# The up product of an expert stage in 128 + 64 features, with the last 64 in row tiles

## The chip, the cores and the metric

The kernel runs on one core of a Trainium2 chip. Its time is the device time in microseconds of one execution. The engines are PE (TensorE, with PEld for its weight loads), DVE (VectorE), ACT (ScalarE), POOL (GpSimd) and SP (SyncE, which here only issues DMAs). They run side by side and wait for each other through semaphores.

## The reference

One layer over 16 images, 256 tokens each, 192 features: a tokenizer, attention with 12 heads, and a mixture of 16 experts of which each token uses two. The change touches the mixture alone:

```python
logits = jnp.einsum('bld,ed->ble', x, Wr)
probs = jax.nn.softmax(logits, axis=-1)
top_p, top_idx = jax.lax.top_k(probs, TOP_K)                 # TOP_K = 2
gating = jnp.sum(jax.nn.one_hot(top_idx, N_EXPERTS) * top_p[..., None], axis=-2)
def step(y, params):
    W1e, b1e, W2e, b2e, ge = params                          # 192x768, 768, 768x192, 192
    h = jax.nn.gelu(jnp.einsum('bld,df->blf', x, W1e) + b1e, approximate=False)
    out = jnp.einsum('blf,fd->bld', h, W2e) + b2e
    return (y + ge[..., None] * out, None)
```

All of it is in fp32.

## The kernel before

The program has three parts. The image stage (to about 535 us) runs 16 images through tokenizer, attention and router logits. The routing stage (to about 600 us) sorts the 8192 pairs of token and expert by expert into 79 tiles of 128 rows; each tile belongs to one expert, and its number stands in the table `tab`. `r_new` says whether a tile's expert differs from that of the tile two before, whose weight buffer it takes over. The expert stage (to about 991 us) works through the 79 tiles; a last part adds each token's two results.

The expert stage has no planner. Each engine runs its own written list, and semaphores tie them. For tile t:

- POOL gathers the tile's 128 rows of 192 features from `x2_d` in DRAM into `xt` (L594), and later scatters the results to `pair_d` (L600). Four buffers each.
- SP (`moe_loads`) reads expert number and flag into registers (L309, L315) and issues the loads of w1, b1 (`first`, L320 and L323) and w2, b2 (`second`, L328 and L332) into one of two buffers. With the flag at 0 the DMA moves nothing. `first(t)` waits for the up product of t-2 and `second(t)` for the down product of t-2 and its bias sum.
- PE (`moe_tensor`) transposes the rows (`rows_T`, L380, two halves of 96 features), does the up product (`up`, L391 and L392) and the down product (`down`, L402). Its order is up(t), rows_T(t+1), down(t-1), up(t+1).
- The up product has six chunks of 128 hidden units. Each is two matmuls: 96 features, and 96 features and a row of ones, which brings in the bias b1 that lies below w1 as row 97. Both accumulate into the same place of PSUM.
- ACT applies gelu to all 768 columns at once (L429). DVE copies the transposed rows to SBUF (L545) and adds b2 to the down product (L553).

SP, PE, ACT and DVE run this stage as a loop over four tiles at a time, with some tiles written out ahead of and behind it. DMAs that SP issues share one queue, in order.

Of the kernel before, what the change touches and what calls it, by code (L numbers as in the profile page):

```python
# [15 lines left out]
def vit_tower(nc, x0, x1, x2, w0t, w1t, w2t, b012, wft, bf, idx0, idx1, idx2, w_qkv, w_out, b_out, ln_g, ln_b,  # L16
# [3 lines left out]
    ds = bass.ds  # L20

    P = 128
# [29 lines left out]
    x2_d = nc.dram_tensor("x2_rows", ((NT + 1) * P, E), fp32).ap()  # L52
# [4 lines left out]
    qk_d = nc.dram_tensor("qk_parts", (2, 2, NPART, E, T), bf16).ap()  # L57
    NTOK, FIRST = NT * P, NT * P + P
# [3 lines left out]
    with ctx:  # L62
# [45 lines left out]
        def carve(memory, size):  # L108
# [3 lines left out]
            def part(shape, dt=fp32):  # L112
# [11 lines left out]
                if len(shape) == 2:  # L124
# [59 lines left out]
        padrow = sb("padrow", [P, E])  # L184
# [40 lines left out]
        w1b = [late([KH + 1, 2, FF]) for p in range(2)]  # L225
        w2b = [late([P, FC, E]) for p in range(2)]
        b2b = [late([P, E]) for p in range(2)]
        NB = 4
        xt = [late([P, E]) for b in range(NB)]
# [4 lines left out]
        xtT = [late([KH + 1, 2, P]) for p in range(2)]  # L234
# [7 lines left out]
        H = [BK[:, 2 * p:2 * p + 2, :].rearrange("p b n -> p (b n)")[:, 0:FF] for p in range(2)]  # L242
# [12 lines left out]
                 "out_done").split()  # L255
# [46 lines left out]
        def tile_at(k, n):  # L302

            return k + n // 4, n % 4

        def moe_loads(sp):
            sp.wait_ge(s["r_tab"], 1)
            def expert(t):
                return sp.value_load(tab[0:1, ds(t, 1)], min_val=0, max_val=NE - 1)  # L309

            def fresh(t):

                if isinstance(t, int) and t < 2:
                    return None
                return sp.value_load(r_new[0:1, ds(t, 1)], min_val=0, max_val=1)  # L315

            def first(t, p):
                e, new = expert(t), fresh(t)
                wait_prev(sp, s["m_s1"], t - 1)
                sp.dma_start(w1b[p][0:KH, :, :], ew1[ds(e, 1), :, :].rearrange("a (c p) f -> p (a c) f", p=KH),  # L320
                             cond=new) \
                    .then_inc(s[f"m_wa{p}"], 16)
                sp.dma_start(w1b[p][KH:KH + 1, 1, :], eb1[ds(e, 1), :], cond=new).then_inc(s[f"m_wa{p}"], 16)  # L323

            def second(t, p):
                e, new = expert(t), fresh(t)
                wait_prev(sp, s["m_s2"], t - 1)
                sp.dma_start(w2b[p][:, :, :], ew2[ds(e, 1), :, :].rearrange("a (c p) d -> p (a c) d", p=P),  # L328
                             cond=new) \
                    .then_inc(s[f"m_wb{p}"], 16)  # L330
                wait_prev(sp, s["m_y"], t - 1)
                sp.dma_start(b2b[p][:, :], eb2[ds(e, 1), :].rearrange("a d -> (a d)").partition_broadcast(P),  # L332
                             cond=new) \
                    .then_inc(s[f"m_b{p}"], 16)


            first(0, 0)
            for t in range(2):
                first(t + 1, (t + 1) % 2)
                second(t, t % 2)  # L340
            with sp.Fori(0, (NTILE - 3) // 4) as k:
                for j in range(4):
                    first(4 * k + j + 3, (j + 1) % 2)
                    second(4 * k + j + 2, j % 2)
            second(NTILE - 1, (NTILE - 1) % 2)
# [14 lines left out]
        def moe_tensor(pe):  # L360
# [14 lines left out]
            def rows_T(q, r):  # L375
                t, p = 4 * q + r, r % 2
                pe.wait_ge(s[f"m_x{r}"], 16 * q + 16)
                wait_prev(pe, s["m_xT"], t - 1)
                for c in range(2):
                    last = nc.tensor.matmul(XT[p][0:KH, c * P:(c + 1) * P], xt[r][:, c * KH:(c + 1) * KH],  # L380
# [3 lines left out]
            def up(q, r):  # L384
                t, p = 4 * q + r, r % 2
                pe.wait_ge(s["m_xT"], t + 1)
                pe.wait_ge(s[f"m_wa{p}"], 64 * q + 32 * (r // 2) + 32)
# [8 lines left out]
            def down(q, r):  # L396
                t, p = 4 * q + r, r % 2
                pe.wait_ge(s["m_gelu"], t + 1)
                pe.wait_ge(s[f"m_wb{p}"], 32 * q + 16 * (r // 2) + 16)
                wait_prev(pe, s["m_y"], t - 1)  # L400
                for c in range(FC):
                    last = nc.tensor.matmul(Y[p], hT[p][:, c * P:(c + 1) * P], w2b[p][:, c, :],  # L402
                                            start=(c == 0), stop=(c == FC - 1))
                last.then_inc(s["m_s2"], 1)

            rows_T(0, 0)
            rows_T(0, 1)
            up(0, 0)
            up(0, 1)
            rows_T(0, 2)  # L410
            down(0, 0)
            with pe.Fori(0, (NTILE - 3) // 4) as k:
                for j in range(4):
                    up(*tile_at(k, j + 2))
                    rows_T(*tile_at(k, j + 3))
                    down(*tile_at(k, j + 1))
            up(*tile_at(0, NTILE - 1))
            down(*tile_at(0, NTILE - 2))
            down(*tile_at(0, NTILE - 1))

        def moe_scalar(act):
# [3 lines left out]
            def gelu(q, r):  # L425
                t, p = 4 * q + r, r % 2
# [4 lines left out]
            for t in range(3):  # L431
                gelu(0, t)
            with act.Fori(0, (NTILE - 3) // 4) as k:
                for j in range(4):
                    gelu(*tile_at(k, j + 3))

        def moe_vector(dve):
# [12 lines left out]
            for p in range(2):  # L450
                V.memset(xtT[p][KH:KH + 1, :, :], 1.0)
# [20 lines left out]
            V.tensor_copy(r_pad[:, :], padid_i[:, :])  # L472
            V.tensor_copy(r_id[:, 0, :], tokid_i[:, :])
# [37 lines left out]
            for c in range(PAIRS // CG):  # L511
                b, at = c % 2, slice(c * CG, (c + 1) * CG)
                if c == 2:
# [5 lines left out]
                    V.tensor_tensor(r_new[:, 2:NTILE], r_tf[:, 2:NTILE], r_tf[:, 0:NTILE - 2], ALU.not_equal)  # L519
# [21 lines left out]
            def rows_T(q, r):  # L541
                t, p = 4 * q + r, r % 2
                dve.wait_ge(s["m_tr"], t + 1)
                wait_prev(dve, s["m_s1"], t - 1)
                V.tensor_copy(xtT[p][0:KH, :, :], XT[p][0:KH, 0:2 * P].rearrange("p (c t) -> p c t", c=2)) \  # L545
                    .then_inc(s["m_xT"], 1)

            def biased(q, r):
                t, p = 4 * q + r, r % 2
                dve.wait_ge(s["m_s2"], t + 1)  # L550
                dve.wait_ge(s[f"m_b{p}"], 32 * q + 16 * (r // 2) + 16)
                wait_prev(dve, s[f"m_sc{r}"], 16 * q)
# [840 lines left out]
```

## Time and profile before

| | |
|---|---|
| median of 3 runs | 1026.74 us (1025.71 to 1027.69) |
| profiled execution | 1025.64 us, its span 1023.8 us |
| PE busy | 841.7 us, 82% |
| PEld busy | 716.0 us, 70% |
| DVE, ACT, POOL busy | 384.2, 289.1, 398.3 us |
| chain that ended last, largest shares | L402 13%, L391 9%, L392 9% |

The page cuts the span into 40 slices of 25.6 us. PE's digits are 9 (90% or more busy) in slices 6 to 19 and 25 to 38: most of the image stage, and the expert stage. The granted clock is 9 in tenths in both and 5 in the routing stage between them. Queue 1 holds SP's DMAs (84.49 MB), queue 0 POOL's (17.90 MB), and the two instruction queues brought 31 packets of program code, 0.38 MB, for 0.1% of the 16 DMA engines' time. Instructions on PE overlap: a matmul's duration in a row is longer than the distance to the next start, and it is the distances that fill the stage.

### The profile page before, as it was taken

Reading aid. Unit: us, or ns where it says so; the run is one execution under the profiler, and the core shown is the slowest. Engines: PE = TensorE matmul, PEld = TensorE weight load, DVE = VectorE, ACT = ScalarE, POOL = GpSimd, SP = SyncE. Lnnn points to the kernel's source line nnn. Section 1 sums busy time; section 2 is a strip of 40 time slices with the busy share of each in tenths; the row PEclk is TensorE's granted clock in tenths of the full one; section 3 lists DMA queues with packets and bytes.
Section 4 is the critical chain, followed back from the end, with each engine's and each line's share of the span. In section 5 each row is a group of like instructions: output and inputs, shape, how many; then the busy total and the mean of one; then the engine's idle time right before and its main releaser. Section 6 shows DMA issues by size and latency. Waiting matters only on the chain. (4 is left out here: it accounts for less than half of the span.)

```text
span 1023.8 us, 19480 instructions
## 1 busy us (share of the span) xinstructions
PE 841.7 (82%) x6395; PEld 716.0 (70%) x6396; DVE 384.2 (38%) x816; ACT 289.1 (28%) x466; POOL 398.3 (39%) x585
## 2 busy tenths in 40 slices
PE   0047899999999999999740879999999999999970
PEld 0025566666666666676430879999999999999960
DVE  3000355555555555556439911111111111111118
ACT  0011455555555555555310001111111111111110
POOL 7720234444444444444330533433443344334410
PEclk9999999999999999999855569999999999999995
DMA  7203233333333333333011227252367655465129
GB/s 216 34 5 72 70 73 74 73 73 72 72 72 72 72 72 72 72 70 73 1 77 46 75 58 202 69 142 73 104 166 190 169 157 169 120 187 167 42 62 330
DMA packets 83517, 102.78 MB, mean 100 GB/s; under 512 B 14639, under 2 KB 69152, under 8 KB 83294
## 3 DMA queue, kind: packets, MB, share of 16 engines
q1 hardware_dynamic: 74334, 84.49, 31.6%
q0 software_dynamic: 9152, 17.90, 6.3%
q8 instruction: 16, 0.26, 0.1%
q14 instruction: 15, 0.12, 0.0%
HBM read 139.67 MB, written 25.17 MB: 161 GB/s over the span
## 5 line engine op out<-in xcount | busy, mean ns | idle before, releaser
L391 PE MATMUL BK<-shared 96*128 96x128 f32 x948 | 185.0, 276 | 0.7 <-issue 0.6
L392 PE MATMUL BK<-shared 97*128 97x128 f32 x948 | 184.4, 276 | 0.0
L429 ACT ACTIVATE shared<-BK 128x768 f32<-128x768 f32 x79 | 64.0, 810 | 385.1 <-PE BK L392 385.1
L402 PE MATMUL BK<-shared 128*128 128x192 f32 x948 | 168.0, 325 | 1.1 <-DMA shared<-ew 1.1
L600 POOL DMA_INDIRECT pair_rows<-shared x79 | 78.0, 987 | 217.2 <-DVE shared L553 212.9
L402 PEld LDWEIGHTS BK<-shared 128*128 128x128 f32 x948 | 153.1, 190 | 1.4 <-DMA shared<-ew 1.4
L391 PEld LDWEIGHTS BK<-shared 96*128 96x128 f32 x948 | 148.5, 192 | 1.7 <-issue 0.8
L392 PEld LDWEIGHTS BK<-shared 97*128 97x128 f32 x948 | 144.9, 192 | 0.0
L1136 DVE TENSOR_REDUCE negmax<-BK 128x6 f32<-128x1536 f32 x64 | 112.1, 1751 | 10.8 <-PE BK L792 10.6
L545 DVE COPY shared<-BK 96x256 f32<-96x256 f32 x79 | 33.3, 421 | 203.7 <-PE BK L380 203.7
L1011 ACT ACTIVATE shared<-BK 128x1536 f32<-128x1536 f32 x64 | 92.6, 1446 | 24.4 <-PE BK L813 24.2
L594 POOL DMA_INDIRECT shared<-x_rows,shared x79 | 76.7, 971 | 30.2 <-issue 23.8
L553 DVE TENSOR_TENSOR shared<-BK,shared 128x192 f32<-128x192 f32 x79 | 28.2, 357 | 129.4 <-PE BK L402 129.4
L1109 DVE COPY hr<-BK 128x384 f32 (+1 forms) x16 | 8.9, 557 | 170.3 <-PE BK L754 170.3
L824 PE MATMUL BK<-shared,v 128*32 128x256 f32 x768 | 69.1, 385 | 3.9 <-ACT oT L1017 2.4
L772 PE MATMUL BK<-x1T,wqkv 96*96 96x256 f32 x256 | 67.0, 408 | 5.5 <-DVE shared L1128 4.5
L714 PE MATMUL BK<-ident,xs 16*96 16x16 f32 (+1 forms) x192 | 18.9, 224 | 58.5 <-POOL xs L1261 57.8
L792 PE MATMUL BK<-shared 96*128 96x256 bf16 x384 | 54.6, 280 | 6.3 <-DVE negmax L1136 4.0
L714 PEld LDWEIGHTS BK<-ident,xs 16*96 16x96 f32 (+1 forms) x192 | 13.8, 125 | 64.2 <-issue 62.6
L772 PEld LDWEIGHTS BK<-x1T,wqkv 96*96 96x96 f32 x256 | 41.8, 174 | 21.3 <-DVE shared L1128 8.3
L813 PE MATMUL BK<-shared 99*128 99x256 bf16 x384 | 53.3, 275 | 0.9 <-ACT shared L1011 0.9
L792 PEld LDWEIGHTS BK<-shared 96*128 96x128 bf16 x384 | 35.1, 100 | 25.6 <-DVE negmax L1136 10.7
(153 smaller groups left out, 1143.1 us busy)
## 6 DMA issues: line engine op xcount, KB each, us to landing
shared<-ew SPq DMA_DIRECT2D x158, 576.0 KB
shared<-qk_parts SPq DMA_DIRECT2D x112, 96.0 KB, 3.3
qk_parts<-shared SPq DMA_DIRECT2D x32, 288.0 KB, 2.9
shared<-eb SPq DMA_DIRECT2D x79, 96.0 KB
shared<-qk_parts SPq DMA_DIRECT2D x16, 288.0 KB, 3.7
shared<-qk_parts SPq DMA_DIRECT2D x16, 192.0 KB, 4.1
x_rows<-xrow SPq DMA_DIRECT2D x1, 3072.0 KB, 8.7
xrow<-pair_rows SPq DMA_DIRECT2D x8, 384.0 KB, 8.2
```

What stands on the lines that cost most here:

```text
L391: nc.tensor.matmul(o, w1b[p][0:KH, 0, c * P:(c + 1) * P], xtT[p][0:KH, 0, :], start=True, stop=False)
L392: last = nc.tensor.matmul(o, w1b[p][:, 1, c * P:(c + 1) * P], xtT[p][:, 1, :], start=False, stop=True)
L402: last = nc.tensor.matmul(Y[p], hT[p][:, c * P:(c + 1) * P], w2b[p][:, c, :], start=(c == 0), stop=(c == FC - 1))
L429: nc.scalar.activation(hT[p][:, :], H[p], ACT.Gelu).then_inc(s["m_gelu"], 1)
L594: nc.gpsimd.indirect_dma_start(xt[t % NB][:, :], None, x2_d, bass.IndirectOffsetOnAxis(t_src[:, t:t + 1], 0)) \
L600: nc.gpsimd.indirect_dma_start(pair_d, bass.IndirectOffsetOnAxis(t_dst[:, t:t + 1], 0), ysum[t % NB][:, :], None).then_inc(s[f"m_sc{t % NB ...
L772: last = nc.tensor.matmul(M0[0:KH, h * T:(h + 1) * T], wqkv[:, c, at:at + KH], x1T[:, c, :], start=(c == 0), stop=(c == 1))
L792: last = nc.tensor.matmul(S[:, a, t * T:(t + 1) * T], qs[p][0:KS, h, t * P:(t + 1) * P], ks[p][0:KS, h, :], start=True, stop=True)
L813: last = nc.tensor.matmul(ST[:, a, t * T:(t + 1) * T], ks[p][:, h, t * P:(t + 1) * P], qs[p][:, h, :], start=True, stop=True)
L824: last = nc.tensor.matmul(M1[32 * a:32 * a + 32, 0:T], v[p][:, t, HU * u + a, :], pT[u % 2][:, a, t * T:(t + 1) * T], start=(t == 0), stop ...
L1011: nc.scalar.activation(pT[u % 2][:, :, :], ST[:, :, :], ACT.Exp).then_inc(s["act_exp"], 1)
L1136: nc.vector.tensor_reduce(negmax[:, :, HU * u:HU * u + HU].rearrange("p t h -> p h t"), S[:, :, :].rearrange("p a (t k) -> p a t k", t=TT) ...
```

## The change

The up product contracts 192 features as 128 + 64 rather than 96 + 97.

- The first 128 features (`w1a`) are one full matmul per chunk, six in all.
- The other 64 features (`w1c`) use half of the array's rows. `w1c` holds them for chunks 0 to 2 on partitions 0 to 63 and for chunks 3 to 5 on partitions 64 to 127. The matmuls go in pairs, one on the upper and one on the lower half of the array (row tiles), into two PSUM banks. To make such a layout loadable, two DMAs at the start of the program write the last 64 rows of every w1 into a table `w1c_d` in DRAM, 3 MB.
- The transposed rows must lie on both halves. So `x2_d` has rows of 256: 192 features and the last 64 once more, stored by two DMAs. The gather fetches 256 values, and each transpose is 128 wide.
- b1 leaves the product. Behind the routing, six small matmuls of b1 (`b1r`) with a one-hot table of the tiles' experts (`b1e`) give `b1t`, 128 x 6 x 79, which stays in SBUF. ACT adds it in the gelu, which is therefore six instructions of 128 columns, since each chunk has its own bias column.
- SP, PE, ACT and DVE have the 79 tiles written out, without loops. SP reads a tile's number and flag once instead of twice.

PE, one tile in the expert stage. Names: L391 and L392 are the two halves of the up product, L380 the transposes, L402 the down product. Before:

```order
L391 MATMUL BK<-shared 128x128
L392 MATMUL BK<-shared 128x128
L377 ISA
L299 REGISTER_ALU [waits m_x3]
L380 MATMUL BK<-ident,shared 96x128 [waits m_xT]
L380 MATMUL BK<-ident,shared 96x128
L399 ISA [waits m_gelu]
L402 MATMUL BK<-shared 128x192 [waits m_y,m_wb1]
L402 MATMUL BK<-shared 128x192 x5
L386 REGISTER_ALU
L391 MATMUL BK<-shared 128x128 [waits m_gelu,m_wa1,m_xT]
L392 MATMUL BK<-shared 128x128
```

Now, with L398 the 128 features, L403 the 64, L388 the transposes and L413 the down product:

```order
L398 MATMUL BK<-shared 128x128 [waits m_gelu,m_wa1,m_xT]
L398 MATMUL BK<-shared 128x128 x5
L403 MATMUL BK<-shared 128x128 x6
L388 MATMUL BK<-ident,shared 128x128 [waits m_xT,m_x0]
L388 MATMUL BK<-ident,shared 128x128
L413 MATMUL BK<-shared 128x192 [waits m_y,m_wb0,m_gelu]
L413 MATMUL BK<-shared 128x192 x5
L398 MATMUL BK<-shared 128x128 [waits m_gelu,m_wa0,m_xT]
```

There are twelve matmuls of the up product before and now; they no longer alternate, six of the full array stand first and then six of half the array. The stage's order is otherwise kept.

SP, one tile's loads, L309 and L315 the reads of the table, L320 and L323 w1 and b1, L328 w2, L332 b2. Before:

```order
L309 TENSOR_LOAD shared
L309 ISA x2
L315 ISA
L315 TENSOR_LOAD shared
L315 ISA x2
L299 REGISTER_ALU
L320 ISA [waits m_s1]
L320 DMA shared<-ew 96x2x768
L323 ISA
L323 DMA shared<-eb 1x768
L309 TENSOR_LOAD shared
L309 ISA x2
```

Now, L316 and L317 the reads, L323 and L325 the two parts of w1, L331 w2:

```order
L316 TENSOR_LOAD shared
L316 ISA x2
L317 TENSOR_LOAD shared
L317 ISA x2
L323 ISA [waits m_s1]
L323 DMA shared<-ew 128x768
L325 ISA
L325 DMA shared<-up_rest 128x384
L331 DMA shared<-ew 128x6x192 [waits m_s2]
L335 ISA [waits m_y]
L335 DMA shared<-eb 128x192
```

The second pair of reads between the two halves of the loads is gone, and b1's DMA of one row has become the DMA of `w1c`.

```diff
-    x2_d = nc.dram_tensor("x2_rows", ((NT + 1) * P, E), fp32).ap()
+    x2_d = nc.dram_tensor("x2_rows", ((NT + 1) * P, 2 * P), fp32).ap()
+    KR, HC = E - P, FC // 2
+    w1c_d = nc.dram_tensor("up_rest", (NE, P, FF // 2), fp32).ap()
+    NW = 2
...
-        w1b = [late([KH + 1, 2, FF]) for p in range(2)]
+        w1a = [late([P, FF]) for w in range(NW)]
+        w1c = [late([P, FF // 2]) for w in range(NW)]
...
-        H = [BK[:, 2 * p:2 * p + 2, :].rearrange("p b n -> p (b n)")[:, 0:FF] for p in range(2)]
+        H = [[BK[:, 2 * p + c // HC, c % HC * P:(c % HC + 1) * P] for c in range(FC)] for p in range(2)]
...
+            def first(t, e, new):
+                w = t % NW
+                wait_prev(sp, s["m_s1"], t - NW + 1)
+                sp.dma_start(w1a[w][:, :], ew1[ds(e, 1), 0:P, :].rearrange("a k f -> (a k) f"), cond=new) \
+                    .then_inc(s[f"m_wa{w}"], 16)
+                sp.dma_start(w1c[w][:, :], w1c_d[ds(e, 1), :, :].rearrange("a k f -> (a k) f"), cond=new) \
+                    .then_inc(s[f"m_wa{w}"], 16)
...
+            pe.wait_ge(s["ld_b1"], 16)
+            pe.wait_ge(s["r_hot"], 1)
+            for c in range(FC):
+                last = nc.tensor.matmul(BK[:, 1, c * NTILE:(c + 1) * NTILE], b1r[:, c * P:(c + 1) * P], b1e[:, :],
+                                        start=True, stop=True)
+            last.then_inc(s["pe_b1"], 1)
             pe.wait_ge(s["r_meta"], 1)
+            pe.wait_ge(s["dve_b1"], 1)
...
                 for c in range(FC):
-                    o = H[p][:, c * P:(c + 1) * P]
-                    nc.tensor.matmul(o, w1b[p][0:KH, 0, c * P:(c + 1) * P], xtT[p][0:KH, 0, :], start=True, stop=False)
-                    last = nc.tensor.matmul(o, w1b[p][:, 1, c * P:(c + 1) * P], xtT[p][:, 1, :],
-                                            start=False, stop=True)
+                    nc.tensor.matmul(H[p][c], w1a[w][:, c * P:(c + 1) * P], xtT[p][:, 0, :],
+                                     start=(c % HC == 0), stop=False, skip_group_check=True)
+                for c in range(HC):
+                    for h in range(2):
+                        k = slice(h * KR, (h + 1) * KR)
+                        last = nc.tensor.matmul(H[p][h * HC + c], w1c[w][k, c * P:(c + 1) * P], xtT[p][k, 1, :],
+                                                start=False, stop=True, skip_group_check=True)
                 last.then_inc(s["m_s1"], 1)
...
-                nc.scalar.activation(hT[p][:, :], H[p], ACT.Gelu).then_inc(s["m_gelu"], 1)
+                for c in range(FC):
+                    last = nc.scalar.activation(hT[p][:, c * P:(c + 1) * P], H[p][c], ACT.Gelu, bias=b1t[:, c, t:t + 1])
+                last.then_inc(s["m_gelu"], 1)
...
-            for p in range(2):
-                V.memset(xtT[p][KH:KH + 1, :, :], 1.0)
...
+                    V.tensor_scalar(b1e[:, :], r_tf[0:NE, :], eid[:, 0:1], None, ALU.is_equal).then_inc(s["r_hot"], 1)
...
+            dve.wait_ge(s["pe_b1"], 1)
+            V.tensor_copy(b1t[:, :, :], BK[:, 1, 0:FC * NTILE].rearrange("p (c t) -> p c t", t=NTILE)) \
+                .then_inc(s["dve_b1"], 1)
...
+            sp.dma_start(b1r[:, :], eb1).then_inc(s["ld_b1"], 16)
+            for h in range(2):
+                sp.dma_start(w1c_d[:, h * KR:(h + 1) * KR, :], ew1[:, P:E, h * (FF // 2):(h + 1) * (FF // 2)]) \
+                    .then_inc(s["st_w1c"], 16)
...
-            sp.dma_start(x2_d[0:NT * P, :].rearrange("(p t) e -> p t e", t=NT), xrow[:, :, :]).then_inc(s["st_x2"], 16)
+            rows = x2_d[0:NTOK, :].rearrange("(p t) e -> p t e", t=NT)
+            sp.dma_start(rows[:, :, 0:E], xrow[:, :, :]).then_inc(s["st_x2"], 16)
+            sp.dma_start(rows[:, :, E:2 * P], xrow[:, :, P:E]).then_inc(s["st_x2"], 16)
```

## Rows read from the trace of the kernel before

**Rows 1.** Table by stretches, expert stage: busy us (count) per engine, TensorE clock, DMA share, GB/s.

```profile
620.00:1000.00 380.00, 369.54 (x2873) 368.33 (x2871) 60.62 (x157) 61.52 (x76) 145.85 (x149) 0.99 0.48 135
```

**Rows 2.** List of waits, 599 to 1000 us, PE: us in total, times, longest.

```profile
PE BK L380 <- DMA shared<-x_rows,shared: 5.4, 2, 4.8
PE BK L402 <- DMA shared<-ew: 1.1, 1, 1.1
```

**Rows 3.** Instructions in order of time, one tile: start us, us, instruction, count, [idle before].

```profile
764.54 0.39 PE L391 MATMUL BK<-shared 96*128 96x128 f32 x2
...
767.22 0.38 PE L380 MATMUL BK<-ident,shared 128*96 128x128 f32 x2
...
767.45 2.13 PE L402 MATMUL BK<-shared 128*128 128x192 f32 x12
...
769.41 0.39 PE L391 MATMUL BK<-shared 96*128 96x128 f32 x2
```

**Rows 4.** Instructions in order of time, image stage, PE around L824.

```profile
302.21 0.41 PE L824 MATMUL BK<-shared,v 128*32 128x256 f32 x2
302.26 0.22 PE L737 MATMUL BK<-w2s,x12T 96*16 96x64 f32 x1
302.32 1.03 PE L824 MATMUL BK<-shared,v 128*32 128x256 f32 x10
...
308.48 1.06 PE L824 MATMUL BK<-shared,v 128*32 128x256 f32 x12
309.48 0.83 PE L792 MATMUL BK<-shared 96*128 96x256 bf16 x6
```

**Rows 5.** The same stretch from 303.27 us: three tile shapes in a row, PE and PEld.

```profile
303.27 0.70 PE L744 MATMUL BK<-rr,bd 128*128 128x256 f32 x2
303.90 0.65 PE L745 MATMUL BK<-rr,bd 128*64 128x256 f32 x2
304.48 0.64 PE L714 MATMUL BK<-ident,x2c 128*96 128x128 f32 x4
...
303.90 0.19 PEld L745 LDWEIGHTS BK<-rr,bd 128*64 128x64 f32 x2 [0.33 <-issue]
```

**Rows 6.** The same view, 299 us: PEld where 64 rows follow 128.

```profile
299.12 0.69 PEld L714 LDWEIGHTS BK<-ident,xs 64*96 64x96 f32 x10 [0.20 <-issue]
```

**Rows 7.** The page's groups of instructions: busy us, mean ns of one, idle before.

```profile
L429 ACT ACTIVATE shared<-BK 128x768 f32<-128x768 f32 x79 | 64.0, 810 | 385.1 <-PE BK L392 385.1
...
L545 DVE COPY shared<-BK 96x256 f32<-96x256 f32 x79 | 33.3, 421 | 203.7 <-PE BK L380 203.7
...
L1011 ACT ACTIVATE shared<-BK 128x1536 f32<-128x1536 f32 x64 | 92.6, 1446 | 24.4 <-PE BK L813 24.2
...
L824 PE MATMUL BK<-shared,v 128*32 128x256 f32 x768 | 69.1, 385 | 3.9 <-ACT oT L1017 2.4
```

**Rows 8.** Instructions in order of time: SP's DMA issues, first load, a skipped one, a real one.

```profile
572.14 0.37 SPq L320 DMA_DIRECT2D shared<-ew  x1
...
673.14 0.08 SPq L328 DMA_DIRECT2D shared<-ew  x1
...
763.32 0.33 SPq L320 DMA_DIRECT2D shared<-ew  x1
```

**Rows 9.** The same view, end of routing and first gather.

```profile
587.69 7.25 PE L370 MATMUL BK<-pixels 128*128 128x79 f32 x33
...
596.91 1.07 POOL L594 DMA_INDIRECT shared<-x_rows,shared  x1 [6.43 <-DVE shared L539]
...
599.75 0.64 PE L380 MATMUL BK<-ident,shared 128*96 128x128 f32 x2 [4.81 <-DMA shared<-x_rows,shared]
```

**Rows 10.** Table by stretches: the store of the rows, and a w2b load.

```profile
533.00:541.00 8.00, 1.40 (x7) 1.29 (x7) 5.54 (x11) 1.91 (x2) 0.00 (x0) 0.50 0.92 393
...
679.00:682.00 3.00, 3.00 (x24) 3.00 (x23) 0.42 (x1) 0.81 (x1) 0.97 (x1) 1.00 0.89 257
```

**Rows 11.** Instructions in order of time, start: POOL behind its last gather.

```profile
57.12 0.33 POOL L1260 COPY xs<-pixels 64x192 f32<-64x192 f32 x1 [1.45 <-DMA pixels<-x,i]
```

More of the change, by code:

```diff
@@ L223, in vit_tower @@
         r_new = late([P, NTILE], i32)
-        w1b = [late([KH + 1, 2, FF]) for p in range(2)]
-        w2b = [late([P, FC, E]) for p in range(2)]
-        b2b = [late([P, E]) for p in range(2)]
+        w1a = [late([P, FF]) for w in range(NW)]
+        w1c = [late([P, FF // 2]) for w in range(NW)]
+        w2b = [late([P, FC, E]) for w in range(NW)]
+        b2b = [late([P, E]) for w in range(NW)]
         NB = 4
-        xt = [late([P, E]) for b in range(NB)]
+        xt = [late([P, 2 * P]) for b in range(NB)]
         r_df = late([P, NTILE])
@@ L233, in vit_tower @@
         t_dst = late([P, NTILE], i32)
-        xtT = [late([KH + 1, 2, P]) for p in range(2)]
+        xtT = [late([P, 2, P]) for p in range(2)]
         hT = [late([P, FF]) for p in range(2)]
@@ L299, in wait_prev @@
                 eng.wait_ge(which, count)
-        def tile_at(k, n):
-            return k + n // 4, n % 4
         def moe_loads(sp):
             sp.wait_ge(s["r_tab"], 1)
[L308 to L320, printed above, removed]
-                             cond=new) \
[L322 to L328, printed above, removed]
-                             cond=new) \
[L330 to L345, printed above, removed]
@@ new lines, in moe_loads, with chosen @@
+            sp.wait_ge(s["st_w1c"], 32)
+            def chosen(t):
+                e = sp.value_load(tab[0:1, t:t + 1], min_val=0, max_val=NE - 1)
+                new = None if t < NW else sp.value_load(r_new[0:1, t:t + 1], min_val=0, max_val=1)
+                return e, new
+            def first(t, e, new):
[5 more added lines that the diff above has]
+                    .then_inc(s[f"m_wa{w}"], 16)
@@ new lines, in second @@
+            def second(t, e, new):
+                w = t % NW
+                wait_prev(sp, s["m_s2"], t - NW + 1)
+                sp.dma_start(w2b[w][:, :, :], ew2[ds(e, 1), :, :].rearrange("a (c p) d -> p (a c) d", p=P),
+                             cond=new) \
+                    .then_inc(s[f"m_wb{w}"], 16)
+                wait_prev(sp, s["m_y"], t - NW + 1)
+                sp.dma_start(b2b[w][:, :], eb2[ds(e, 1), :].rearrange("a d -> (a d)").partition_broadcast(P),
+                             cond=new) \
+                    .then_inc(s[f"m_b{w}"], 16)
@@ L347, in moe_loads @@
+            before = chosen(0)
+            first(0, *before)
+            for t in range(1, NTILE):
+                now = chosen(t)
+                first(t, *now)
+                second(t - 1, *before)
+                before = now
+            second(NTILE - 1, *before)
             for b in range(NB):
@@ L378, in rows_T @@
+            def rows_T(t):
+                p, r = t % 2, t % NB
+                pe.wait_ge(s[f"m_x{r}"], 16 * (t // NB) + 16)
                 wait_prev(pe, s["m_xT"], t - 1)
                 for c in range(2):
-                    last = nc.tensor.matmul(XT[p][0:KH, c * P:(c + 1) * P], xt[r][:, c * KH:(c + 1) * KH],
+                    last = nc.tensor.matmul(XT[p][:, c * P:(c + 1) * P], xt[r][:, c * P:(c + 1) * P],
                                             ident[:, :], start=True, stop=True, is_transpose=True)
@@ L394, in up, with down @@
                 last.then_inc(s["m_s1"], 1)
-            def down(q, r):
-                t, p = 4 * q + r, r % 2
+            def down(t):
+                p, w = t % 2, t % NW
                 pe.wait_ge(s["m_gelu"], t + 1)
-                pe.wait_ge(s[f"m_wb{p}"], 32 * q + 16 * (r // 2) + 16)
+                pe.wait_ge(s[f"m_wb{w}"], 16 * (t // NW) + 16)
                 wait_prev(pe, s["m_y"], t - 1)
                 for c in range(FC):
-                    last = nc.tensor.matmul(Y[p], hT[p][:, c * P:(c + 1) * P], w2b[p][:, c, :],
+                    last = nc.tensor.matmul(Y[p], hT[p][:, c * P:(c + 1) * P], w2b[w][:, c, :],
@@ L403, in down @@
                                             start=(c == 0), stop=(c == FC - 1))
                 last.then_inc(s["m_s2"], 1)
[L406 to L417, printed above, removed]
@@ L418, in moe_tensor @@
-            down(*tile_at(0, NTILE - 2))
-            down(*tile_at(0, NTILE - 1))
+            rows_T(0)
+            rows_T(1)
+            up(0)
+            for t in range(1, NTILE):
+                up(t)
+                if t + 1 < NTILE:
+                    rows_T(t + 1)
+                down(t - 1)
+            down(NTILE - 1)
         def moe_scalar(act):
@@ L423, in moe_scalar @@
             nc.scalar.activation(r_p[:, :, :], r_ls[:, :, :], ACT.Exp).then_inc(s["r_exp"], 1)
-            def gelu(q, r):
-                t, p = 4 * q + r, r % 2
+            act.wait_ge(s["dve_b1"], 1)
+            for t in range(NTILE):
+                p = t % 2
                 act.wait_ge(s["m_s1"], t + 1)
                 wait_prev(act, s["m_s2"], t - 1)
-                nc.scalar.activation(hT[p][:, :], H[p], ACT.Gelu).then_inc(s["m_gelu"], 1)
[L431 to L435, printed above, removed]
+                for c in range(FC):
+                    last = nc.scalar.activation(hT[p][:, c * P:(c + 1) * P], H[p][c], ACT.Gelu, bias=b1t[:, c, t:t + 1])
+                last.then_inc(s["m_gelu"], 1)
         def moe_vector(dve):
```

57 lines of the change are left out of this document (28 added, 29 removed).

## The prediction

> **What bounds the kernel now.** I read the table by stretches first, then the PE waits, then one tile in order of time. In the expert stage (620 to 1000 us) PE works 369.5 of 380 us at full clock, while DVE works 60.6 and ACT 61.5 [rows 1]. PE's waits from 599 us on hold 4.8 us for the first row gather and 1.1 us for one weight load, and little else [rows 2]. So PE's own instruction stream sets the stage's end, and a change is worth what it takes from that stream.
>
> One tile is the distance between two up products: 764.54 to 769.41, 4.87 us [rows 3]. It splits by start times. The trace shows two MATMULs for each fp32 product. Twelve up products take from 764.54 to 767.22 = 2.68 us, or 24 instructions of 0.112. The two transposes take 0.23. The six down products take from 767.45 to 769.41 = 1.96 us, or 0.163 per instruction of 192 columns. That is 0.85 ns a column, so 0.109 at 128 columns and 0.218 at 256: a matmul costs its moving columns, whether 96 or 128 rows are filled.
>
> **The up product after the change.** Six products contract 128 features: 12 instructions x 0.112 = 1.34 us. Six more contract the remaining 64, three in array rows 0 to 63 and three in rows 64 to 127, alternating: again 12 instructions. All hangs on whether the two halves run side by side. No matmul of before does this with row tiles, so the cost per instruction lies between 0.112 (one after another) and 0.056 (fully paired).
>
> The nearest row is the probability-times-value product L824, in three column tiles. Its 12 instructions of 256 columns take 1.06 us [rows 4]; one after another they would take 12 x 0.218 = 2.6. With the last one's duration off (0.385, L824's mean [rows 7]), 0.675 us holds three intervals of 0.225: four waves of three. So tiles do run abreast, in full, for fp32. I take full pairing: 6 waves x 0.112 = 0.67 us. The weak point is the weight load. L824 loads 32 columns, here it is 128, and a 128-column load fills the slot (the up stream shows a load per 0.112 as well [rows 3]). If loads of the two row tiles took turns, nothing would be gained.
>
> TensorE: Matmul & The Clock Gate of the Trainium skill (section Packing small matmuls) says that matmuls start and end strictly in program order. Under it the two instructions of one product would come before the other tile's, so that 12 instructions would need 7 slots, 0.11 us a tile more. The trace disagrees for column tiles: two of L824 start at 302.21, the last L737, which stands ahead of them in the program, at 302.26 [rows 4]. I keep six slots.
>
> **The price of changing the tile shape.** It is paid twice a tile now, and nothing in the expert stage paid it before. Rows 5 show it: L744 (128 columns of weights) to L745 (64) to L714 (96). L744's two instructions take 0.70; less 0.385 for the last one, also of 256 columns, that is 0.32 between starts, where the columns need 0.218: 0.10 of weight load in the open. From the second L744 to L745 it is 0.63 - 0.32 = 0.31, again 0.09 to 0.10 over 0.218: the array empties. For L745 to L714: 0.65 - 0.38 = 0.27, then 0.58 - 0.27 = 0.31, the same 0.09 to 0.10. The weight loader's own rows show holes of 0.33 us [rows 5], and 0.20 where a 64-row product follows a 128-row one [rows 6], so the row height counts as a shape too. Into the row tiles: 0.10 + 0.10. Back, to transposes: 0.10 + 0.05 (a matmul of 128 columns lasts 0.39 - 0.112 = 0.28 [rows 3], so L714's four stand (0.64 - 0.28) / 3 = 0.12 apart against 0.112; only the first start carries the open load, 0.03 for 96 columns, and I book 0.05 for 128). Together 0.35 us. Bounds: 0 if row tiles need no emptying, 0.42 if both ways cost the dear 0.21.
>
> TensorEngine Tiling (Array Packing) of the Trainium skill (section Key Properties) says the same without a number, that a change of tiling mode drains the array; by these rows the drain alone is 0.1 us. It also says that tiles load weights and multiply in parallel, which for row tiles no row here shows.
>
> **Sum per tile.** Saved: six slots of 0.112 = 0.67. Added: 0.35. Net 0.32 us, so the period goes from 4.87 to 4.55, and 79 tiles give 25.3 us.
>
> **What hides the rest.**
> - Gelu: one ACTIVATE of 768 columns, 0.81 us, becomes six of 128. From 768 columns at 810 ns and 1536 at 1446 [rows 7] a column is 0.83 ns and the start 0.17 us, so 0.28 each, 1.7 us a tile. ACT has a 4.55 us period, and between up(t) and down(t) lie a transpose pair, down(t-1) and up(t+1), over 4 us. At the last tile only down(77), 1.96 us, covers it. Cost 0 to 0.2.
> - Weight loads: a buffer is refilled after up(t-2). A real load issues in 0.33 us where a skipped one takes 0.08 [rows 8]. One is issued at 763.32 for the product at 769.41 [rows 3, 8]: 6.1 us, of which 576 KB at 257 GB/s [rows 10] need 2.3 and the way there some more. Bytes stay 576 KB (384 + 192). With two TENSOR_LOADs a tile fewer SP issues earlier, so I book 0; bounds -1 (the 1.1 us of rows 2 goes) and +4, a few expert changes exposed.
> - The bias table: six small products (12 instructions) stand behind the last L370. There 33 instructions take 7.25 us, 0.22 each [rows 9] at the lower clock, so 2.6 us. PE has nothing until the first gather lands at 599.75, 4.8 us later [rows 2, 9]. DVE's copy of 474 columns (about 0.7 us, by the 0.42 of 256 columns [rows 7]) ends about 598.4. Hidden, margin 1.3 us; if late, 1 us. One small DVE operation at the third chunk adds 0.2.
> - The rows now go out as pieces of 768 and 256 bytes. Before, 3 MB went in 8 us at 393 GB/s [rows 10]; the 768-byte loads run at 257 GB/s, 334 pieces a us. 8192 pieces are then 25 us, from 533 to 558, and the first weights are issued only at 572.14 [rows 8]. Hidden; if pieces of 256 bytes are twice as dear, the first weights wait, up to 5 us.
> - The start: 3 MB go from DRAM to DRAM behind the constants (from about 11 us). PE waits for POOL's gathers, whose last lands at 57.12 [rows 11]. At 257 GB/s for either direction that is 12 to 25 us, so it ends by 36, and what SP has queued behind it (the second level's detour) by about 50. Cost 0, upper bound 10.
>
> Total: 1025.64 (the profiled execution: 1023.8 span and 1.8 around it) - 25.3 + 0.2 = 1000.5 us. The median of the runs shown is 1.1 above that execution.
>
> **Rivals.**
> 1. Slower: the row tiles don't pair, because their 128-column weight loads take turns at 0.112. Then the up product keeps its 2.68 us and the 0.35 for the shape changes comes on top: 79 x 0.35 = 27.7, so 1053.5 us. It decides from 0.17 us a pair: six pairs of that cost 1.01, and with 0.35 the gain is gone. For it: the load fills its slot already, and L824's loads are a quarter as wide. Against: three L824 loads of different tiles fit beside one wave without a trace of turns. 17 in 100.
> 2. Pairs one slot out of step (strict order, two instructions of one product in a row): 7 slots, +0.11 x 79 = 8.8, 1009 us. Against it speaks the overtaking in rows 4. 6 in 100.
> 3. The gain is met by another bound: weights late at the expert changes (16 experts, two buffers each), or straight-line code of 79 tiles that must be fetched. Before, 31 packets of the instruction queues took 0.1% of 16 engines, 16 us, 0.5 each; 30 more, all waited for, are 16 us. The last image steps are straight-line as well, and PE's slice 19, which lies in them, still reads 9. 1005 to 1025; 6 in 100.
> 4. The mechanism is half as dear as I read (no emptying between row shapes): -0.2 x 79, 985 us. 3 in 100.
>
> My forecast has 68 in 100, with 994 to 1006 as its own range. The stated range is 988 to 1030, which takes in rivals 2 and 3 and leaves out rival 1. A measurement of this kernel tells 0.2%, about 2 us, from no change. Faster 0.81 (all but rival 1 and a stray 2), same 0.02, slower 0.17.
>
> **What the profile after would show.** Right: L403 in pairs, two starts within some 10 ns, waves 0.11 apart; one start distance near 0.2 before the first L403 and another after the last; tile period 4.55; no PE wait on gelu or weights; PE's first matmul still near 57.8. Wrong: L403 starts 0.11 apart one by one (rival 1), or period 4.55 with the stage beginning later than 602, or holes of PE in regular distances of three tiles (code).

## The result and the profile after

The changed kernel takes 1000.68 us (median of 4 runs, 998.83 to 1001.66) against 1026.62 us (4 runs) of the kernel before: ratio 0.9745, 95% interval 0.9728 to 0.9762. The forecast was 1000.5. The profiled execution took 998.83 us with a span of 997.0, 26.8 less than before's.

In the changed kernel L398 is the up product over 128 features and L403 that over the last 64, in row tiles. L388 are the transposes, L413 is the down product, L437 gelu, L552 the copy of the transposed rows, L377 the bias table's product. L323, L325, L331 and L335 are SP's loads of w1a, w1c, w2b and b2b. First PE's waits from 600 us on, then SP's (us in total, times, longest), then SP's in the kernel before (there L320 loads w1 and L328 w2):

```profile
PE BK L388 <- DMA shared<-x_rows,shared: 2.7, 2, 2.2
PE BK L413 <- ACT shared L437: 0.3, 1, 0.3
PE BK L398 <- issue: 0.2, 1, 0.2
```

```profile
SPq L331 <- PE BK L413: 99.2, 76, 3.8
SPq L323 <- PE BK L403: 47.9, 48, 30.2
```

```profile
SPq L320 <- PE BK L392: 35.8, 21, 28.3
SPq L328 <- PE BK L402: 7.2, 15, 2.9
```

PE still sets the pace: its wait for a weight load in [rows 2] is gone, and the gather's is shorter because the bias table now fills part of it. SP waits for PE's down product in 76 of 79 tiles, so it is ahead with its loads. Before, it did so in 15.

One tile in order of time (start us, us, instruction, count, idle before), which answers to [rows 3]:

```profile
761.86 1.50 PE L398 MATMUL BK<-shared 128*128 128x128 f32 x12
...
763.29 0.75 PEld L403 LDWEIGHTS BK<-shared 64*128 64x128 f32 x12
763.29 0.94 PE L403 MATMUL BK<-shared 64*128 64x128 f32 x12
...
764.16 0.44 PE L388 MATMUL BK<-ident,shared 128*128 128x128 f32 x2
...
764.28 1.66 ACT L437 ACTIVATE shared<-BK,b1t 128x128 f32<-128x128 f32 x6 [2.88 <-PE BK L403]
...
764.44 2.13 PE L413 MATMUL BK<-shared 128*128 128x192 f32 x12
...
766.43 1.58 PE L398 MATMUL BK<-shared 128*128 128x128 f32 x12
```

Below, a slot is the 0.11 us between two starts of a stream, a wave is what starts in one slot, and a visit is the way into the row tiles and back out. Twelve instructions of L403 take 0.94 us with the last one's own 0.27, so their starts lie within 0.67; L398's twelve lie within 1.23. Single records say how. The last L398 starts at 763.088, two L403 at 763.292 and .299, the next two at .506 and .512, then pairs at .618, .729, .841 and .952, each with its partner 7 ns behind. The first transpose follows at 764.161, the second at .328, the down product at .437. Those are six waves. Four distances exceed the 0.11 of a stream: 0.204 into the first wave (+0.092), 0.214 between the first two (+0.103), 0.202 out of the last (+0.092), and 0.167 between the transposes (+0.057). The sum is 0.344 us a visit, all of it at the change of shape.

The page's groups (busy us, mean ns, idle before), which answer to [rows 7]:

```profile
L437 ACT ACTIVATE shared<-BK,b1t 128x128 f32<-128x128 f32 x474 | 131.0, 376 | 222.4 <-PE BK L403 222.4
...
L403 PE MATMUL BK<-shared 64*128 64x128 f32 x948 | 74.4, 289 | 0.0
...
L403 PEld LDWEIGHTS BK<-shared 64*128 64x128 f32 x948 | 59.3, 187 | 9.7 <-issue 0.2
```

The same 948 matmul records on 64 rows occupy 74.4 us, where L398's 948 on 128 rows occupy 120.0, at almost one mean (289 and 276 ns). PEld shows that loads of 128 columns pair too: 948 loads of 187 ns in 59.3 us of busy time, where L398's 948 of 193 ns fill 117.0.

A tile's period is the distance between the starts of two tiles' first down products. In the two profiled executions it is 4.87 us before and 4.54 after. The parts of the span:

```
stretch                                           before   after   difference
start to the end of the image stage               535.30  534.72      -0.57
end of the image stage to the last one-hot chunk   59.68   61.71      +2.03
last chunk to the first up product                  6.45    6.56      +0.11
first up product to the first down product          7.92    6.99      -0.93
78 tile periods: 78 x 0.327                                          -25.51
  what single periods take beyond that               2.89    0.66     -2.23
  the last two periods, which are shorter           -3.12   -2.75      +0.37
first down product of the last tile to final stage   9.73    9.77      +0.04
final stage                                         25.37   25.25      -0.12
```

The end of the image stage is the first routing maximum on DVE, the end of the chunks the DVE instruction that reads them, the final stage begins with its first DVE addition. The rows sum to the span's -26.8. The 2.89 us stand at six periods of one trace: 2.37 of them at the second to fifth, where the first expert changes lie. Between the first up product and the first down product stand two up products, the first of them mostly at a granted clock of 0.50 (to 606.3 us in both), so this part gives 0.93 and not twice 0.33.

### The profile page after: what moved, and what is told of

Its sections match the earlier page's. It is cut to its first block and busy times, and to the rows that moved or that the text cites. A ratio compares the mean times of both kernels' runs of the same rounds, so it can differ in the third digit from the quotient of the medians.

```text
span 997.0 us, 18493 instructions
## 1 busy us (share of the span) xinstructions
PE 818.0 (82%) x6408; PEld 673.0 (67%) x6408; DVE 383.8 (38%) x817; ACT 356.4 (36%) x861; POOL 400.4 (40%) x586
## 5 line engine op out<-in xcount | busy, mean ns | idle before, releaser
L437 ACT ACTIVATE shared<-BK,b1t 128x128 f32<-128x128 f32 x474 | 131.0, 376 | 222.4 <-PE BK L403 222.4
L413 PE MATMUL BK<-shared 128*128 128x192 f32 x948 | 168.1, 326 | 0.3 <-ACT shared L437 0.3
L413 PEld LDWEIGHTS BK<-shared 128*128 128x128 f32 x948 | 153.1, 190 | 0.7 <-ACT shared L437 0.6
L398 PE MATMUL BK<-shared 128*128 128x128 f32 x948 | 120.0, 276 | 0.2 <-issue 0.2
L398 PEld LDWEIGHTS BK<-shared 128*128 128x128 f32 x948 | 117.0, 193 | 0.7 <-issue 0.5
L552 DVE COPY shared<-BK 128x256 f32<-128x256 f32 x79 | 33.6, 425 | 178.1 <-PE BK L388 178.1
L403 PE MATMUL BK<-shared 64*128 64x128 f32 x948 | 74.4, 289 | 0.0
L403 PEld LDWEIGHTS BK<-shared 64*128 64x128 f32 x948 | 59.3, 187 | 9.7 <-issue 0.2
L1297 POOL TENSOR_TENSOR nm<-negmax,ones 128x12 bf16<-128x12 f32 x32 | 6.8, 212 | 116.9 <-DVE negmax L1145 116.9
```

The lines of the kernel that those rows point to most:

```text
L398: nc.tensor.matmul(H[p][c], w1a[w][:, c * P:(c + 1) * P], xtT[p][:, 0, :], start=(c % HC == 0), stop=False, skip_group_check=True)
L403: last = nc.tensor.matmul(H[p][h * HC + c], w1c[w][k, c * P:(c + 1) * P], xtT[p][k, 1, :], start=False, stop=True, skip_group_check=True)
L437: last = nc.scalar.activation(hT[p][:, c * P:(c + 1) * P], H[p][c], ACT.Gelu, bias=b1t[:, c, t:t + 1])
```

## Experiments

**1. Don't let the halves pair.** All six 64-feature products in array rows 0 to 63; the second half of the hidden columns then takes its remaining weights from the first half.

```diff
-                        k = slice(h * KR, (h + 1) * KR)
+                        k = slice(0, KR)
```

> All six products of 64 features use array rows 0 to 63 (chunks 3 to 5 are computed with the weights of chunks 0 to 2, so half of the hidden units are wrong). If the gain comes from pairs that run abreast: the twelve instructions stand 0.11 apart, 0.66 us more a tile, period 5.20 and 1053 us. If the pairing is not what gains (the weights only arrive earlier, say): no change, 1001.

1054.04 us (one run; before on that chip 1028.08), period 5.20. In order of time:

```profile
762.41 1.60 PE L403 MATMUL BK<-shared 64*128 64x128 f32 x12
763.94 0.44 PE L388 MATMUL BK<-ident,shared 128*128 128x128 f32 x2
```

1.60 us instead of 0.94: twelve slots instead of six, exactly the 0.66 us of pairing, and the shape changes are unmoved. This is the stream of rival 1, though not for rival 1's reason, and its period is within 0.02 of that rival's 4.87 + 0.35. That the time lands on the rival's 1053.5 as well is partly chance, since the image stage ended 2.5 us later here than in the changed kernel's profile.

**2. Take the row tiles away.** The same six products over all 128 rows, which adds both halves' products.

```diff
-                        k = slice(h * KR, (h + 1) * KR)
+                        k = slice(0, P)
```

> The second six products take all 128 rows (the sums then hold the other half's features too, so the hidden units are wrong). No change of the tile shape is left, and no pairs. If a round trip between the shapes costs 0.34 us a tile: period 4.54 + 0.66 - 0.34 = 4.86, 1026 us, against 1053 of the run with one half. If changing the shape is free and only the first weight load shows: 1041. If it costs nothing at all: 1053.

1032.81 us, period 4.86. The period is the expected one; the time is 6.8 above the expected 1026, and the image stage of this one run ended 9.9 us later than that of the changed kernel's profile.

```profile
762.78 1.50 PE L398 MATMUL BK<-shared 128*128 128x128 f32 x12
764.12 1.50 PE L403 MATMUL BK<-shared 128*128 128x128 f32 x12
765.46 0.38 PE L388 MATMUL BK<-ident,shared 128*128 128x128 f32 x2
765.68 2.13 PE L413 MATMUL BK<-shared 128*128 128x192 f32 x12
```

From the first L398 to the first L388 it is 2.68 us, 24 slots of 0.112 without a gap. Against experiment 1 the period falls by 0.34: the price of one visit to the row tiles, measured by itself.

It also bears on the stalls. It has before's pace (4.86 against 4.87) and the changed kernel's loads, and its periods hold 0.10 us too much where before's hold 2.89. So the faster PE isn't what removed them. Eight traces with the changed kernel's loads (the changed kernel's two, experiments 1 to 4, 6 and 11) hold 0 to 0.9 us and experiment 5's holds 1.6, against 2.89 in the one trace of before. That points at what changed for the loads. Whether the single reading of the table, the missing DMA of b1 or the lists without loops did it was not taken apart.

**3. More visits.** Two full products of L400 and a pair of L404, three times over; nothing else differs. The edit in short, with `full` and `pair` for the products of one chunk:

```diff
-                for c in range(FC): full(c)
-                for c in range(HC): pair(c)
+                for c in range(HC):
+                    full(c); full(HC + c)
+                    pair(c)
```

> The same products, but after every two full ones their pair of halves: three visits to the row tiles in a tile instead of one. If each visit costs 0.34 us: two more are 0.69 a tile, 54 us, 1055 us, period 5.23. If the price is that of the first visit alone, or is hidden behind a queue of full products: 1001.

1067.06 us, period 5.33:

```profile
764.02 0.60 PE L400 MATMUL BK<-shared 128*128 128x128 f32 x4
764.55 0.49 PE L404 MATMUL BK<-shared 64*128 64x128 f32 x4
764.98 0.71 PE L400 MATMUL BK<-shared 128*128 128x128 f32 x4
765.62 0.49 PE L404 MATMUL BK<-shared 64*128 64x128 f32 x4
766.04 0.71 PE L400 MATMUL BK<-shared 128*128 128x128 f32 x4
766.68 0.49 PE L404 MATMUL BK<-shared 64*128 64x128 f32 x4
767.10 0.44 PE L388 MATMUL BK<-ident,shared 128*128 128x128 f32 x2
```

Two visits more cost 0.79, 0.39 each, where 0.34 was expected (period 5.23, 1055 us). The mechanism holds, and the size depends on what follows: the first L400 group takes 0.60, those that come back from a row tile 0.71, so a full product pays 0.10 more on return, where the transposes pay 0.057. In single records a visit that ends in a full product costs 0.092 + 0.103 us in and 0.091 + 0.102 out.

**4. One half after the other.** The two loops swapped, so the three products of rows 0 to 63 stand in the program ahead of the three of rows 64 to 127.

```diff
-                for c in range(HC):
-                    for h in range(2):
+                for h in range(2):
+                    for c in range(HC):
```

> The same products, the three of the upper half first and then the three of the lower half, no longer alternating. If PE starts matmuls strictly in the order of the program: 11 or 12 slots of 0.11 instead of 6, up to 0.66 us more a tile, 1044 to 1053 us. If each row tile has its own queue, as the overtaking of L737 by L824 suggests: still pairs, 1001. I hold the two about equal; between them, a limited reach, 1010 to 1040.

1027.6 us, period 4.86:

```profile
762.41 1.26 PE L403 MATMUL BK<-shared 64*128 64x128 f32 x12
```

The starts: 762.415, .628, .741 and .747, .852, .960 and .964, 763.072 and .075, and .183, .296, .407 alone. The records don't name the half, but the first instruction of a half shows by its own duration (0.373 in place of 0.27 us), and it is the one at .415 and the one at .747. So the second half does overtake, but begins only when the third instruction of the first has started, with three of the first still to come. Its second instruction is 0.21 behind its first, as in the first half. It so ends three slots after the first half: nine slots in place of six (3 x 0.11 = 0.33, and the periods differ by 0.32). Of the recorded expectations this is the one between, a limited reach. Pairing thus needs neighbours in the program: the engine reached about three instructions ahead here.

**5. Two gelu instructions instead of six.** 384 columns each, the first bias left out.

```diff
-                for c in range(FC):
-                    last = nc.scalar.activation(hT[p][:, c * P:(c + 1) * P], H[p][c], ACT.Gelu, bias=b1t[:, c, t:t + 1])
+                for c in range(2):
+                    last = nc.scalar.activation(hT[p][:, c * HC * P:(c + 1) * HC * P],
+                                                BK[:, 2 * p + c, 0:HC * P], ACT.Gelu)
```

> The gelu of a tile in two instructions of 384 columns without the bias b1 (b1 is left out of the result). ACT then has about 1.0 us a tile instead of 1.66. If ACT is hidden: 1001, the difference to the changed kernel under 1 us (the first and the last tile only). If gelu's six pieces hold PE up: 3 us or more less.

1003.35 us (1000.73 to 1003.73; ratio to before 0.9731, 0.9691 to 0.9771), period 4.54. ACT's two instructions of 0.49 us take the place of 1.66 us a tile and the period doesn't move: gelu is hidden. PE's one wait of 0.3 us for gelu, at the first down product, is absent here.

**6. Move the small DVE operation.** The +2.03 us of the routing had no term in the forecast beside 0.2. In the changed kernel one instruction is new in that stretch: L523, the table of hot columns b1e, ahead of the third one-hot chunk. Moved behind the last one:

```diff
-                    V.tensor_scalar(b1e[:, :], r_tf[0:NE, :], eid[:, 0:1], None, ALU.is_equal).then_inc(s["r_hot"], 1)
...
+            V.tensor_scalar(b1e[:, :], r_tf[0:NE, :], eid[:, 0:1], None, ALU.is_equal).then_inc(s["r_hot"], 1)
             dve.wait_ge(s["oh_pe"], PAIRS // CG)
```

> The one-hot table of the tiles' experts is computed behind the last chunk of the routing instead of in its third. In the changed kernel the routing's chunks end 2.0 us later than before although only 0.17 us of DVE work was added: there two POOL multiplications take 5.2 us where they took 2.15 each. If the shift of DVE against POOL causes that: the first gather is issued about 2 us earlier, 998.7 us. If it is chance of another kind: unchanged, 1001.

The stretch is back at 59.68 us; in experiments 1 to 5, with the instruction where the change put it, it was 61.7. The time, 1001.64 (999.03 to 1004.2; 0.9714, 0.9674 to 0.9755), can't tell 2 us from nothing, so both kernels were run on one chip:

> The changed kernel itself, beside its variants on the same chip. 1000.7 us or the chip's own value, ratio to the kernel before 0.9745; its stretch from the end of the image stage to the end of the chunks 61.7 us. It is the yardstick for the other two of this call.

> The changed kernel with only the table of hot columns moved behind the last one-hot chunk, this time beside the changed kernel. Theory (the 2.0 us that the routing lost are VectorE and GpSimd meeting in another phase): stretch 59.7 us again, first up product 1.6 to 2.0 us earlier, time 2 us (0.2%) below the changed kernel. Rival (the stretch is on the trace of one execution only, or the time is given back at the first tile, whose gather or bias table then ends last): first up product at most 0.5 us earlier, time the same.

Changed kernel 1002.67 us (1001.25 to 1005.21; 0.9757, 0.9722 to 0.9792), with b1e later 998.66 us (997.54 to 999.95; 0.9711, 0.968 to 0.9742), four runs each. The stretches are 61.72 and 59.69 us, and from the end of the image stage to the first up product it is 68.32 and 66.25. Nothing is given back later: first up product to final stage takes 368.9 and 368.3. The medians lie 4.0 us apart, of which the traces give 2.07 to this stretch; their image stages end 0.85 us apart, which the move doesn't explain. Every run of this version was faster than every run of the changed kernel on this chip, by 0.4% in the median, though the intervals of the two ratios to before overlap.

The third and fourth chunk in order of time, DVE and POOL, in the first profile of the changed kernel:

```profile
570.44 0.24 DVE L523 TENSOR_SCALAR b1e<-shared,eid 16x79 f32<-16x79 f32 x1
570.61 0.80 DVE L526 TENSOR_TENSOR pixels<-iota,shared 128x632 f32<-128x632 f32 x1
...
571.49 4.03 POOL L586 TENSOR_TENSOR pixels<-pixels,shared 128x632 f32<-128x632 f32 x1 [4.42 <-DVE pixels L526]
572.47 0.80 DVE L526 TENSOR_TENSOR pixels<-iota,shared 128x632 f32<-128x632 f32 x1
573.20 1.21 DVE L531 TENSOR_TENSOR pixels<-iota,shared 128x1024 f32<-128x1024 f32 x1
...
575.48 1.24 POOL L586 TENSOR_TENSOR pixels<-pixels,shared 128x632 f32<-128x632 f32 x1
575.55 1.84 DVE L526 TENSOR_TENSOR pixels<-iota,shared 128x632 f32<-128x632 f32 x1 [1.14 <-POOL pixels L586]
```

and with b1e later (experiment 11):

```profile
573.40 0.81 DVE L525 TENSOR_TENSOR pixels<-iota,shared 128x632 f32<-128x632 f32 x1
574.13 1.22 DVE L530 TENSOR_TENSOR pixels<-iota,shared 128x1024 f32<-128x1024 f32 x1
574.29 2.16 POOL L586 TENSOR_TENSOR pixels<-pixels,shared 128x632 f32<-128x632 f32 x1 [4.26 <-DVE pixels L525]
575.26 1.85 DVE L525 TENSOR_TENSOR pixels<-iota,shared 128x632 f32<-128x632 f32 x1
```

When DVE builds the fourth chunk's 128x632 compare beside POOL's multiply of the third, one of them is slowed. With b1e later it is DVE (1.85 in place of 0.81) and POOL keeps 2.16. In the changed kernel DVE keeps 0.80 and runs its next compare too, and POOL's multiply takes 4.03. PE waits for that multiply: its first product of the third chunk starts 5.05 us after the chunk's compare, against 3.19 with b1e later. These 1.86 us and the 0.17 by which the new instruction delays DVE are the 2.03.

In both kernels POOL's multiply ends 1.1 us after one of DVE's 128x1024 compares has ended: of L530, from 574.13 to 575.35, and of L531, from 573.20 to 574.41. That looks as if the two engines take turns and POOL missed one, but no run here tests it. That the place of b1e causes the 2 us is shown. What decides which engine yields is not: in both kernels the fourth compare starts 0.97 to 0.98 us behind POOL's multiply.

**7 to 9. Share a visit between two tiles.** If a visit costs 0.34 to 0.39, two tiles that make it together save 0.17 to 0.20 each. Order on PE: full products of t and t+1, then both tiles' pairs, four transposes, down(t-1), down(t). The edit in short:

```diff
+            for t in range(0, NTILE, 2):
+                for u in both: up_full(u)
+                for u in both: up_half(u)
+                for u in (t + 2, t + 3): rows_T(u)
+                for u in (t - 1, t): down(u)
```

The first with two buffers for each weight, the second with three for w1, the third with three for w1, w2 and b2 and with b1e later (the hidden rows moved to the memory of the pixels to make room).

> Two tiles share one visit to the row tiles: full products of t and t+1, halves of t and t+1, transposes of t+2 and t+3, down products of t-1 and t; the lists of DVE, POOL and SP follow. Half of the round trips go: 0.17 a tile, 13.6 us. But a w1 buffer is now refilled within 5.2 us instead of 6.4. If the loads still fit: 987 us. If they don't at the expert changes: some 15 changes by 0.5 to 2 us, 995 to 1015.

> The same with three w1 buffers, so that no load of w1 has less than 6.4 us; one more DVE operation of 0.2 us in the routing. If the round trips are the only difference: 987 us, and at least as fast as with two buffers. If the third buffer's additional loads (one per expert) disturb: 990 or more.

> Two tiles to one visit of the row tiles as before, now with three buffers for every expert tensor (w1, w2 and the second bias; the hidden rows moved to the memory of the pixels to make room) and the table of hot columns formed after the last one-hot chunk. Theory (each visit costs 0.34 us; what ate the gain of the two runs before was the late second weight, whose buffer came free only 6.9 us ahead of its use, and the late issue of it on SP): pair of tiles 8.72 us against 2 x 4.54, down products no longer wait for loads, stage 14 us shorter than the changed kernel's, image-to-expert stretch 2 us shorter: ratio to the changed kernel's time about 0.984, so some 985 us where the changed kernel takes 1001. Rival (the loads themselves, of which there are more with three buffers, keep the DMA engines from serving the gathers in time): pair 8.72 with 8 to 14 us of waits, time 993 to 1001.

1012.53 us (1007.85 to 1016.5; 0.9813, 0.9767 to 0.986), 1008.51 (1005.01 to 1016.83; 0.9765, 0.9726 to 0.9803) and 1006.86 (999.22 to 1010.15; 0.9821, 0.9789 to 0.9852). The expectation of 987 us failed for the first two; the time of the first lies in its rival's 995 to 1015. An undisturbed pair takes 8.72 us against 2 x 4.54 in all three, 0.36 less, so the visit's price is confirmed once more. But the gain of 14 us is not seen. All three are slower than the changed kernel. PE's waits from 600 us on, of the first and of the third (`issue` stands where the profile names no releaser):

```profile
PE BK L406 <- issue: 13.2, 15, 2.5
PE BK L424 <- issue: 3.5, 6, 1.1
```

```profile
PE BK L405 <- issue: 6.9, 7, 1.5
PE BK L423 <- issue: 3.7, 4, 1.4
```

L406 and L405 are the first up products, L424 and L423 the down products. The lost time stands at single tiles, which fits late weight loads, and DMA traffic rises with the buffers; the page of the first and of the third:

```profile
DMA packets 96091, 110.07 MB, mean 108 GB/s; under 512 B 19250, under 2 KB 82483, under 8 KB 95955
```

```profile
DMA packets 113114, 127.96 MB, mean 128 GB/s; under 512 B 20145, under 2 KB 97714, under 8 KB 112978
```

A load is skipped when the expert of tile t is that of tile t minus the number of buffers, so a third buffer makes skips rarer: 17.9 MB more, the weight of 30 loads of 0.59 MB. Over undisturbed pairs the periods hold about 26, 18 and 16 us too much. The third version's stage (371.4 us from first up product to final stage) stays above the 368.9 of the changed kernel and the 368.3 of the one with b1e later, both on the same chip. That more buffers cut the waits and more loads bring some back is the likely reading, not a shown one. The expectation of the third run (985 us) failed, and its median lies above its rival's 993 to 1001 too. Whether the remaining waits come from the DMA engines' load or from the order of issue on SP stays open.

## Why the prediction was right

- **PE's stream is the bound.** Right. Span -26.8, of which tile periods -25.5, and experiments 1 to 4 move the time with PE's period.
- **Pairing, 6 x 0.112 saved.** Right: 0.66 in experiment 1. The weak point named there, loads of 128 columns that would take turns, did not come true; loads of the two tiles overlap like the matmuls (59.3 us busy against 117.0).
- **Shape changes, 0.35 a tile.** Right to 0.01: 0.344 in single records, 0.34 in experiment 2, and the parts too (0.092 + 0.103 in, 0.092 + 0.057 out, forecast 0.10 + 0.10 and 0.10 + 0.05). The rows of the image stage, other shapes of the same engine, were a good source. One reading was weaker than it looked. The loads ahead of [rows 6] are these:

```profile
298.70 0.21 PEld L714 LDWEIGHTS BK<-ident,xs 128*48 128x48 f32 x2
```

  So the weights' columns change there together with the rows (48 to 96), and that hole of 0.20 didn't show that row height alone counts as a shape. The 0.204 and 0.202 us here do, since L398, L403 and L388 all have 128 columns.
- **Period 4.55.** Measured 4.54.
- **Program order.** The prediction weighed the Trainium skill, TensorE: Matmul & The Clock Gate, section Packing small matmuls, by which starts follow the program. In the changed kernel both instructions of one product stand ahead of the partner's, yet the partners start 7 ns apart in six slots, not seven. Experiment 4 shows the overtaking, and that it has a limit.
- **Gelu, bias table, start.** Hidden, as forecast. Experiment 5 shows it for gelu, for which PE waited 0.3 us once. DVE's copy of the table ended at 599.86, the first gather was waited for until 601.41: margin 1.55 (forecast 1.3). PE's first matmul comes at 58.06, before at 57.8.
- **Code without loops (part of rival 3).** The instruction queues brought 38 + 30 packets in place of 31, and PE's list of waits holds no more than 0.2 us without a named releaser.
- **Weight loads, booked 0 with bounds -1 and +4.** Off: what periods take beyond the usual fell by 2.2 us, more than the lower bound allowed. That bound was the 1.1 us in [rows 2]; the same list of before held two more entries:

```profile
PE BK L391 <- issue: 0.6, 1, 0.6
PE BK L391 <- DMA shared<-eb: 0.2, 1, 0.2
```

  That is 1.9 us, and the periods held 2.9: a wait counts only from the modelled end of the last matmul. Counting periods would have given the bound.
- **One small DVE operation, booked +0.2.** This step failed in size: it cost 2.0. The work of 0.2 was priced (0.17 by experiments 6 and 11), the 1.86 us by which POOL's multiply beside DVE grew were not.

These two nearly cancel (-2.2, and +1.8 over what was booked). The image stage's -0.57 lies among what differs from run to run (it ended at 537 to 545 us in the experiments). The sum was made for a profiled execution, and that one came out at 998.83, 1.7 below it; that the median meets it within 0.2 is luck, that the period does within 0.01 is not.

## What to carry to other kernels

A contraction that leaves half of the array's rows empty is worth pairing in row tiles if the saved slots exceed the visit: here 0.34 to 0.39 us each time the shape goes there and back, so put many pairs into one visit and write partners next to each other (4.54 us a tile here, 4.86 with the halves apart). In a chain of engines, price a small added instruction not by its duration but by what it moves out of step behind it, and look whether it can stand where its engine waits. Before merging steps further, count what a new buffer count does to the loads that are skipped now.

## What the runs showed of the hardware

- Two fp32 products on 64 rows each run side by side in full, weight loads of 128 columns included: starts 7 ns apart, 0.11 us a wave of 128 columns.
- A change between 128 and 64 rows costs 0.092 us each way beyond the usual slot (the first start after it is 0.202 to 0.204 us off). To that comes the first weight load in the open: 0.10 for a product, 0.057 for a transpose, both of 128 columns.
- An instruction of the other row tile starts ahead of older ones. In experiment 4 it did so with three of them still to start, not with four.
- A compare of 128x632 on DVE beside a multiply of the same size on POOL: 1.85 us and 2.16, or 0.80 and 4.03, with the starts equally far apart (0.97 and 0.98 us).
